# Joined score calls, earlier maxima and exponentials, and PSUM banks by expected end of reading, in a decoder's cross attention

## What is computed

```python
q = (queries @ wq_w + wq_b).reshape(B, S, H, DK)            # H = 16, DK = 64, S = 256
k_ext = concat([keys @ wk_w + wk_b, mk])                    # 256 + 128 = 384 keys
v_ext = concat([values @ wv_w + wv_b, mv])
scores = einsum('bhsd,bhtd->bhst', q, k) / sqrt(DK)
out = einsum('bhst,bhtd->bhsd', softmax(scores), v)
x = _layernorm(x + out @ wo_w + wo_b)
```

## Time and profile before

| | us |
|---|---|
| median of 3 runs | 1592.1 |
| lowest and highest run | 1581.37, 1595.23 |
| the profiled execution | 1586.94 |
| its span, first to last instruction | 1585.2 |

### The profile page before, as it was taken

One profiled execution on the slowest core, in us unless ns is written; L12 is line 12 of the kernel. 1 busy time (PEld: TensorE's weight loads), 2 busy tenths in 40 slices (PEclk: granted clock), 3 DMA queues, 4 the chain that ended last, 5 costly groups with the idle time before them and its releaser, 6 DMA issues.

```text
span 1585.2 us, 27670 instructions
## 1 busy us (share of the span) xinstructions
PE 1390.1 (88%) x9268; PEld 1122.7 (71%) x9268; DVE 1102.7 (70%) x2434; ACT 934.6 (59%) x2307; POOL 822.9 (52%) x862
## 2 busy tenths in 40 slices
PE   4778999999999999956999999689999979997891
PEld 3556777777777777654999999345555548997881
DVE  4677876666666666557788874688899963666635
ACT  4666565655655655542688861367778834466653
POOL 3664454444444444432688862287778750074640
PEclk9888999999999999956999999889999986998996
DMA  4100000000000000036556668634344402244574
GB/s 146 41 28 7 28 8 8 2 8 1 8 8 1 8 2 1 1 142 259 186 209 214 240 207 303 228 113 155 121 140 138 141 23 81 87 167 160 198 243 177
DMA packets 52942, 167.85 MB, mean 106 GB/s; under 512 B 13178, under 2 KB 22340, under 8 KB 44996
## 3 DMA queue, kind: packets, MB, share of 16 engines
q1 hardware_dynamic: 45316, 145.63, 26.1%
q0 software_dynamic: 7488, 20.46, 4.1%
HBM read 149.28 MB, written 16.78 MB: 105 GB/s over the span
## 4 chain that ended last, share of the span: by engine, by line
PE 34%; DVE 8%; issue 5%; ACT 5%; POOL 4%; DMA 2%; POOLq 0%; DVEq 0%; ACTq 0%; SPq 0%
PE m_ps L1713 10%; PE m_ps L1736 9%; POOL s_hc L2010 2%; DVE s_h L2345 2%; PE m_ps L1710 2%; PE s_yps L2410 2%; PE m_ps L1731 2%; ACT s_dps L2081 1%; PE m_ps L1693 1%; PE m_ps L1633 1%; DMA m_xrow<-table,m_row_from 1%; PE s_yps L2497 1%; PE m_ps L1643 1%; DVE tokens L1600 1%; PE m_ps L1661 1%
## 5 line engine op out<-in xcount | busy, mean ns | idle before, releaser
L306 POOL TENSOR_TENSOR a_pexp<-a_pexp,a_rsum 128x384 f32<-128x384 f32 (+1 forms) x320 | 246.0, 787 | 303.5 <-DVE a_rsum L523 303.5
L396 ACT ACTIVATE a_pexp<-a_ps,a_nmax 128x384 f32<-128x384 f32 (+1 forms) x320 | 180.8, 565 | 171.8 <-DVE a_nmax L519 171.3
L1713 PE MATMUL m_ps<-m_xT,m_w1s 128*128 128x256 f32 x1344 | 211.7, 296 | 18.0 <-issue 14.7
L1736 PE MATMUL m_ps<-m_w2s,m_hs 128*128 128x256 f32 x1344 | 203.4, 288 | 1.9 <-DVE m_hs L1532 1.9
L519 DVE TENSOR_REDUCE a_nmax<-a_ps 128x1 f32<-128x384 f32 (+1 forms) x320 | 153.8, 522 | 71.8 <-PE a_ps L620 70.7
L1713 PEld LDWEIGHTS m_ps<-m_xT,m_w1s 128*128 128x128 f32 x1344 | 186.4, 201 | 22.1 <-issue 17.3
L1736 PEld LDWEIGHTS m_ps<-m_w2s,m_hs 128*128 128x128 f32 x1344 | 181.5, 196 | 2.8 <-DVE m_hs L1532 1.7
L2010 POOL TENSOR_TENSOR s_hc<-s_h,s_bc_rows 128x1024 f32<-128x1024 f32 x64 | 150.9, 2361 | 61.0 <-DVE s_h L2345 59.0
L1096 POOL DMA_INDIRECT m_xrow<-table,m_row_from x78 | 81.5, 1044 | 142.0 <-DVE m_row_from L1431 107.0
L2345 DVE TENSOR_TENSOR_SCAN s_h<-s_dps,s_inp 128x512 f32<-128x512 f32 x128 | 148.7, 1203 | 0.0
L636 PE MATMUL a_ps<-a_ident,a_pexp 128*128 128x128 f32 x896 | 144.7, 274 | 3.4 <-ACT a_pT L255 3.0
(11 more groups left out here) (402 smaller groups left out, 3409.7 us busy)
## 6 DMA issues: line engine op xcount, KB each, us to landing
s_bc_rows<-s_bc_table SPq DMA_DIRECT2D x64, 512.0 KB, 3.7
arrived<-in_down SPq DMA_DIRECT2D x29, 1024.0 KB, 6.5
arrived<-in_up SPq DMA_DIRECT2D x23, 1024.0 KB
m_w<-in_up SPq DMA_DIRECT2D x24, 512.0 KB
m_w<-in_down SPq DMA_DIRECT2D x24, 512.0 KB
arrived<-results SPq DMA_DIRECT2D x3, 1024.0 KB, 8.4
m_fin<-results SPq DMA_DIRECT2D x4, 768.0 KB
tokens<-in_x SPq DMA_DIRECT2D x8, 256.0 KB, 6.8
```

Of the source, the lines that this page charges most:

```text
L306: nc.gpsimd.tensor_tensor(pexp[:, r, 0:n], pexp[:, r, 0:n], rsum[:, r:r + 1].to_broadcast([128, n]), ALU.mult).then_inc(normed, 1)
L396: nc.scalar.activation(pexp[:, r, 0:n], ps_s[score_bank(u)][:, 0:n], ACT.Exp, bias=nmax[:, r:r + 1], accum_out=sums[:, r:r + 1]).then_inc( ...
L1713: last = nc.tensor.matmul(ps_hid[ft % RING], w1s[wb][wp][:, k, of], xT[:, j % 2, xp, k, :], start=(k == 0 and wp == 0 and xp == 0), stop=( ...
L1736: last = nc.tensor.matmul(ps_y[j % 2][:, s, :], hs[hp][:, ft % RING, s * 128:(s + 1) * 128], w2s[wb][wp][:, ft, :], start=(ft == 0 and s = ...
```

## The change

1. In cross attention two score calls are joined: `scores(v)` and `scores(v + 2)` are both issued at the first step of a group, twelve matmuls in a row, and four banks (0 to 3) take them.
2. The maxima of the group's units 2 and 3 move from step 2 to step 1, and the exponentials of units 2 and 3 from steps 2 and 3 to steps 1 and 2.
3. T, pv and the jobs share banks 4 to 7 in cross attention. The planner gives out the bank whose reading it expects to end first, at 1.8 steps after a job's last part, 1.9 after a T and 2.3 after a pv. In self attention T has bank 4 and pv bank 3 (before 3 and 4).
4. q4, q5 and q6 move from steps 11, 16 and 17 to 6, 8 and 11, q7 from 18 to 17, x1T from 19 to 18.

```diff
-        ps = [ctx.enter_context(nc.psum_tensor(f"a_ps{n}", [128, 512], fp32)) for n in range(8)]
-        ps_s, PT_BANK, LAST_PT_BANK = ps[0:3], 3, 4
+        ps_all = ctx.enter_context(nc.psum_tensor("a_ps", [128, 8, 512], fp32))
+        ps = [ps_all[:, n, :] for n in range(8)]
+        SELF_PT_BANK, SELF_PV_BANK = 4, 3
...
-        score_bank = lambda u: u % 3
+        score_bank = lambda u: u % 3 if u < NS else u % 4
...
-        pt_bank = lambda n: ps[PT_BANK if n < NS // 2 else PT_BANK + n % 2]
...
+        def scores_at(v):
+
+            return (v,) if 0 <= v < NS and v % 2 == 0 else (v, v + 2) if NS <= v < UNITS and v % 4 == 0 else ()
+
+        def maxima_at(v):
+
+            if 0 <= v < NS:
+                return (v, v + 1) if v % 2 == 0 else ()
+            return {0: (v, v + 1), 1: (v + 1, v + 2)}.get(v % 4, ()) if NS <= v < UNITS else ()
+
+        def exponentials_at(v):
+
+            if 0 <= v < NS:
+                return (v,)
+            return {0: (v,), 1: (v, v + 1), 2: (v + 1,), 3: ()}[v % 4] if NS <= v < UNITS else ()
...
-            for at, kind, b in ((0, "k6", i), (1, "k7", i), (2, "q3", i), (11, "q4", i), (16, "q5", i), (16, "ctxT", i + 1), (17, "q6", i),
-                                (18, "q7", i), (19 if i >= 0 else 17, "x1T", i + 1), (19, "k0", i + 1), (20, "k1", i + 1), (21, "k2", i + 1), (22, "k3", i + 1),
+            for at, kind, b in ((0, "k6", i), (1, "k7", i), (2, "q3", i), (6, "q4", i), (8, "q5", i), (11, "q6", i), (16, "ctxT", i + 1),
+                                (17, "q7", i), (18 if i >= 0 else 17, "x1T", i + 1), (19, "k0", i + 1), (20, "k1", i + 1), (21, "k2", i + 1), (22, "k3", i + 1),
                                 (23, "k4", i + 1), (24, "q0", i + 1), (29, "q1", i + 1), (30, "k5", i + 1), (31, "q2", i + 1)):
...
-        FIXED = {"qk0": 6, "qkT0": 6, "qk1": 7, "qkT1": 7, "xnT": 5, "vs": 5, "oself": 5, "pv": LAST_PT_BANK}
+        FIXED = {"qk0": 6, "qkT0": 6, "qk1": 7, "qkT1": 7, "xnT": 5, "vs": 5, "oself": 5, "pv": SELF_PV_BANK}
...
-        last_in, order, busy_to = {}, {5: -3, 6: -2, 7: -1}, {}
+        last_in, order, read_by = {}, {4: -4, 5: -3, 6: -2, 7: -1}, {}
...
-            for kind, b, part, parts in JOBS_AT.get(v, []) + ([("pv", m, 0, 1)] if m is not None else []):
+            u = pt_at(v)
+            POOLED = (4, 5, 6, 7) if v >= NS + T_LAG else (5, 6, 7)
+            for kind, b, part, parts in JOBS_AT.get(v, []) + ([("pt", u, 0, 1)] if u is not None else []) + ([("pv", m, 0, 1)] if m is not None else []):
                 if part == 0:
-                    if kind in FIXED and v <= SHARED_TO:
+                    if kind == "pt" and u < NS:
+                        bank = SELF_PT_BANK
+                    elif kind in FIXED and v <= SHARED_TO:
                         bank = FIXED[kind]
                     elif v < HELD_TO:
                         bank = 5
                     else:
-                        bank = min((5, 6, 7), key=lambda n: (busy_to.get(n, FIRST) >= v, order[n]))
+                        bank = min(POOLED, key=lambda n: (read_by.get(n, FIRST), order[n]))
                     BANK[kind, b] = bank
                     BEFORE[kind, b] = last_in.get(bank)
                     last_in[bank] = (kind, b)
                     order[bank] = len(BANK)
-                    busy_to[bank] = v + parts - 1
+                    read_by[bank] = v + parts - 1 + {"pt": 1.9, "pv": 2.3}.get(kind, 1.8)
...
+            elif kind == "pt":
+                eng.wait_ge(pt_copied[pt_of(b) % 2], pt_of(b) // 2 + 1)
...
-                    if 0 <= v < UNITS:
-                        exponentials(v)
+                    for u in exponentials_at(v):
+                        exponentials(u)
...
-                    if u >= 2:
-                        pe.wait_ge(exped, u - 1)
+                    if u < NS:
+                        if u >= 2:
+                            pe.wait_ge(exped, u - 1)
+                    else:
+                        pe.wait_ge(exped, max(u - 2, NS))
+                        if u == NS + 2:
+                            pe.wait_ge(o_split, LAST_IN_SELF_PV_BANK + 1)
...
-                    if 1 <= n <= NS // 2:
-                        pe.wait_ge(pt_copied[(n - 1) % 2], (n - 1) // 2 + 1)
-                    elif n == NS // 2 + 1:
-                        pe.wait_ge(o_split, LAST_IN_PT_BANK + 1)
-                    elif n >= 2:
-                        pe.wait_ge(pt_copied[n % 2], n // 2)
+                    if BEFORE["pt", u] is not None:
+                        wait_drained(pe, BEFORE["pt", u])
...
-                    if v % 2 == 0 and 0 <= v < UNITS:
-                        scores(v)
+                    for u in scores_at(v):
+                        scores(u)
```

More of the change, by code:

```diff
@@ L111, in attention_layers @@
         by_nd = lambda a: a.rearrange("p (t d) -> p t d", t=ND)
-        score_bank = lambda u: u % 3
+        score_bank = lambda u: u % 3 if u < NS else u % 4
         pt_of = lambda u: u // 2 if u < NS else NS // 2 + u - NS
         pts_of_pair = lambda m: 2 * m + 2 if m < SELF_PAIRS else NS // 2 + 4 * m + 4 - NS
-        pt_bank = lambda n: ps[PT_BANK if n < NS // 2 else PT_BANK + n % 2]
         keys_of = lambda u: S if u < NS else KEYS
+        assert NS % 4 == 0
+        def scores_at(v):
[8 more added lines that the diff above has]
+            return {0: (v,), 1: (v, v + 1), 2: (v + 1,), 3: ()}[v % 4] if NS <= v < UNITS else ()
         def pt_at(v):
@@ L175, in attention_layers @@
                     order[bank] = len(BANK)
-                    busy_to[bank] = v + parts - 1
-                if part == parts - 1 and kind != "pv":
+                    read_by[bank] = v + parts - 1 + {"pt": 1.9, "pv": 2.3}.get(kind, 1.8)
+                if part == parts - 1 and kind not in ("pt", "pv"):
                     NUMBER[kind, b] = len(NUMBER)
@@ L181, in attention_layers @@
                         HIGH[kind, b] = len(HIGH)
-        LAST_IN_PT_BANK = max(b for kind, b in BANK if kind == "pv" and BANK[kind, b] == LAST_PT_BANK)
+        LAST_IN_SELF_PV_BANK = max(b for kind, b in BANK if kind == "pv" and BANK[kind, b] == SELF_PV_BANK)
         CHUNKS = [("wo0", 0, 2)] + [("wk", c, 5 + 3 * c) for c in range(4)] + [("mk", c, 16 + 2 * c) for c in range(2)] \
@@ L254, in copy_pt @@
             if u < NS:
-                copy(pT[:, m % 2, :, 0:ND, tok(s)], pt_bank(n)[:].rearrange("p (h k s) -> p h k s", h=2, k=ND)).then_inc(pt_copied[n % 2], 1)
+                copy(pT[:, m % 2, :, 0:ND, tok(s)], ps[BANK["pt", u]].rearrange("p (h k s) -> p h k s", h=2, k=ND)).then_inc(pt_copied[n % 2], 1)
             else:
-                copy(pT[:, m % 2, u % 2, :, tok(s)], pt_bank(n)[:, 0:KEYS].rearrange("p (k s) -> p k s", k=KX)).then_inc(pt_copied[n % 2], 1)
+                copy(pT[:, m % 2, u % 2, :, tok(s)], ps[BANK["pt", u]][:, 0:KEYS].rearrange("p (k s) -> p k s", k=KX)).then_inc(pt_copied[n % 2], 1)
         with nc.Block() as block:
@@ L395, in exponentials @@
                         act.wait_ge(pt_raw, pt_of(u - RING) + 1)
-                    nc.scalar.activation(pexp[:, r, 0:n], ps_s[score_bank(u)][:, 0:n], ACT.Exp, bias=nmax[:, r:r + 1],
+                    nc.scalar.activation(pexp[:, r, 0:n], ps[score_bank(u)][:, 0:n], ACT.Exp, bias=nmax[:, r:r + 1],
                                          accum_out=sums[:, r:r + 1]).then_inc(exped, 1)
@@ L515, in _ @@
                     t, r = v // U0, v % U0
-                    if v % 2 == 0 and 0 <= v < UNITS:
-                        for u in (v, v + 1):
-                            dve.wait_ge(scores_raw, u + 1)
-                            nc.vector.tensor_reduce(nmax[:, u % RING:u % RING + 1], ps_s[score_bank(u)][:, 0:keys_of(u)], AX.X, ALU.max, negate=True).then_inc(maxed, 1)
+                    for u in maxima_at(v):
+                        dve.wait_ge(scores_raw, u + 1)
+                        nc.vector.tensor_reduce(nmax[:, u % RING:u % RING + 1], ps[score_bank(u)][:, 0:keys_of(u)], AX.X, ALU.max, negate=True).then_inc(maxed, 1)
                     u = v - R_LAG
@@ L619, in scores @@
                             of = slice(64 * h, 64 * h + 64)
-                            last = nc.tensor.matmul(ps_s[score_bank(u + h)][:, 0:n], q[a][of, tok(s)], k[b][of, :], start=(a == 0 and b == 0), stop=(b == 1))
+                            last = nc.tensor.matmul(ps[score_bank(u + h)][:, 0:n], q[a][of, tok(s)], k[b][of, :], start=(a == 0 and b == 0), stop=(b == 1))
                             if b == 1:
@@ L635, in transpose_weights @@
                         for k in range(keys_of(u) // 128):
-                            last = nc.tensor.transpose(pt_bank(n)[:, at + k * 128:at + k * 128 + 128], pexp[:, g % RING, k * 128:k * 128 + 128], ident[:])
+                            last = nc.tensor.transpose(ps[BANK["pt", u]][:, at + k * 128:at + k * 128 + 128], pexp[:, g % RING, k * 128:k * 128 + 128], ident[:])
                     last.then_inc(pt_raw, 1)
```

## The result

| | before | after |
|---|---|---|
| median of the runs (11 each), us | 1591.72 | 1597.51 |
| the profiled execution, us | 1586.94 | 1594.79 |
| its span, us | 1585.2 | 1593.0 |

The changed kernel is slower by 0.5%: the ratio is 1.0051, with a 95% interval from 1.0032 to 1.0070. In the profiled executions the difference is 7.9 us.

The account below looks back on a forecast made before the run. TensorE issuing its list was taken as the bound (60.74 of 61.77 us busy). Gains 27.5 + 9.4 against losses of some 45 made +8.5 us: 1595.4 profiled, 1600.5 median; own range 1590 to 1611, overall 1572 to 1618.

Parts of the forecast that it names:

- saved per group (G3): Joined score call in each four-step group of cross attention: 0.43 us saved, over 64 groups -27.5 us.
- J1's low part: Low-part reading of the job in a group's second step: to start at 4.87 us, behind two maxima and a second exponential.
- J3: Job of a group's fourth step: takes the second step's job's bank, so starts at 5.41 us instead of 4.38.
- G0, G5, G7: First, sixth and eighth of a batch's eight four-step groups: waits for a low part of 1.03, 1.03 and 0.79 us.
- k0 starts, G4: Job k0 in a batch's fifth group: waits 2.12 us for q7's bank; that group loses 2.79 in all, lasting 9.1.
- light group: Three groups of the last batch, not bound by TensorE: 6.06 us for 5.20, +0.86 three times.
- The first rival: Job readings in cross attention end by 4.38 us, so all new waits go: 36.9 us gained, 1555 us; chance 0.20.
- The second: Second score call in the joined call fills anew: only 0.20 us saved per group, +14.7, 1615 us; chance 0.15.
- G4 of the last batch: Fifth group of the batch without next k and v: predicted to win 0.72 us.
- T3: Transpose of a group's fourth step: comes 1.16 us after the reciprocal behind two maxima; lateness costs a full batch 0.24.
- The two old waits: q4's wait at step 11 and the weighted values' at step 19: both go with the moved jobs, -1.34 us a batch.
- The other stages: Self part and mixture layers outside cross attention: not touched, so a gain or loss passes on whole.

Follow-up runs that it names:

- last experiment: Only the jobs moved, on the kernel before: ratio 0.9997; its reverse, only the jobs moved back, on the changed kernel: 1.0030 of the kernel before.

## Why the prediction was right

The predicted 1600.5 us stands against 1597.51, the predicted 0.5% against 0.5%. By its steps (us):

| step | predicted | measured |
|---|---|---|
| joined call to the next product | 1.23 | 1.27 |
| saved per group (G3) | 0.43 | 0.40 |
| J1's low part starts, G5 | 4.87 | 4.85 |
| J3 starts, G5 | 5.41 | 5.39 |
| G0, G5, G7 | 8.07, 8.07, 7.83 | 8.05, 8.08, 7.81 |
| k0 starts, G4 | 6.12 | 6.05 |
| G4 | 9.1 | 8.94 |
| full batch | 62.9 | 62.6 |
| light group | 6.06 | 6.08 |
| whole kernel, profiled | +8.5 | +7.9 |

Why it came so near: every link of the chain had a row, and the chain is in series, so there was nothing to guess but the order. The part that carried it was to follow the planner's choices to the bank that J3 gets, and to set real times against its steps. The planner counts in steps of equal length; after the join, the two steps from J1 to J3 last 2.08 us, and the two from J3 on nearly 5. The first rival (readings end in time) needed J1's low part at 4.4. It started at 4.85. The second (the call fills anew) needed 1.46 for the joined call.

The misses, all of them small:

- The saving per group. Pairs stand 0.18 apart as predicted, and I took 1.23 where the steps summed to 1.27. 64 groups make 1.9 us less gain.
- G4 of the last batch. Predicted 0.72 shorter than its 6.77 of before, it is 6.71. I had left out that the normalisation at step 16 also delays the maxima there, and with them the reciprocal and T3: 4.19 + 0.65 + 0.42 + 1.44 = 6.70. With the normalisation a step earlier (and the third maximum later) that group is 5.94.
- Batch 0 gained 1.2 us, not 0.3 (59.26 us for 60.44, from one G0 to the next).
- The links of the chain. The prediction says that both maxima stand ahead of J1's low part. Its times need only the first, and the trace shows only that one in the chain, with exponential 2 behind it.
- The two old waits. The prediction has both go by the move of the jobs. The one at step 19 did; the one at step 11 went by the planner's new rule and its pool (last experiment). The 1.34 us fit, but one of their two causes was wrong.
- The other stages. The start of cross attention is 1.7 us earlier (177.82 for 179.56), and what stands behind the start of its last weighted values is 1.8 longer. With the same self part, that start lies between 177.8 and 179.9 in the profiles of the experiments. The two cancel: cross attention alone is 7.7 us longer.
- Two groups lost 1.6 us to the clock (last section); without it cross attention would be 6.2 us longer, where +8.5 was predicted. So terms that were off by one to two us each cancelled in part. The form of the sum is shown by the groups; that the total agrees to 0.6 us is partly luck.

The light group shows the link from the maxima to T3 as the prediction had it, in the order of time of VectorE, GpSimd and TensorE:

```profile
660.60 0.15 DVE L545 RECIPROCAL a_rsum<-a_sums 128x2 f32<-128x2 f32 x1
...
660.83 3.18 POOL L329 TENSOR_TENSOR a_pexp<-a_pexp,a_rsum 128x384 f32<-128x384 f32 x4 [2.90 <-DVE a_rsum L545]
...
661.72 0.55 PE L659 MATMUL a_ps<-a_ident,a_pexp 128*128 128x128 f32 x3 [1.69 <-POOL a_pexp L329]
```

The reciprocal comes 3.04 us after the group's start (657.56), GpSimd 0.23 later, T3 at 4.16. There the earlier maxima hurt: TensorE had idle time in this group already before, so a later T3 makes the group longer at once.

The Trainium skill (TensorEngine Tiling (Array Packing), PSUM Bottleneck) says that tiling speeds up TensorE but not the evacuation of PSUM. Here banks did decide, not matmuls, but not because the readers were full: VectorE was busy 5.27 of 8.08 us in G5 and 6.35 of 8.94 in G4. What lacked was a bank while the chain of readers ran.

## What to carry to other kernels

A planner that gives out buffers by expected end of use should count in time, not in steps, as soon as a change makes the steps unequal (argued from the chain; no run tried such a planner): a join makes the steps behind it short, exactly where buffers come back. When a buffer is taken from a shared pool, walk the longest chain of readers (here maximum, exponential, high part, low part) from the engine that fills it, and see what the in-order engines hold ahead of it; moving instructions behind the reading, here a maximum and two exponentials whose results are needed later, was worth 3 us in 62, and the trace shows exponential 2 as the one that counted (it wasn't moved alone). And a product moved from one full step to another saved nothing, and in the changed kernel it took away what had filled a wait (0.5 us a batch).

## What the runs showed of the chip that I had not expected

In G4 of batch 2 of the changed kernel the wait for q7's low part is as long as in the other batches, but this time the granted clock fell behind it. The wait and the weighted values in TensorE's order of time, and the clock in the windows view:

```profile
336.36 0.39 PE L617 MATMUL a_ps<-a_cT_high,a_wk_high 128*128 128x256 f32 x1 [1.72 <-DVE a_qs_low L499]
...
337.80 2.83 PE L677 MATMUL a_ps<-a_pT,a_vx 128*64 128x256 f32 x12
```

```profile
330.31:336.36 6.05, 4.27 (x38) 3.54 (x36) 4.24 (x11) 4.08 (x13) 2.55 (x4) 1.00 0.15 43
...
337.80:340.56 2.76, 2.76 (x13) 1.38 (x13) 0.95 (x2) 0.05 (x1) 1.51 (x2) 0.50 0.00 0
```

The weighted values ran at 0.50 of the full clock, which is the 1.2 GHz level, and took 2.76 us to the next call for 1.45: a group of 10.25 us for 8.94. The group behind it lost another 0.24 (8.32 for 8.08, granted clock 0.96). Before the fall TensorE had been busy 4.27 of 6.05 us. So this wait, when the clock fell behind it, cost 1.6 us more. It happened once in the seven batches of this profile that have such a G4, each with 1.9 us idle but the first with 1.3. The joined kernel with the old readers (1.9 us idle in G4 or more) shows it in three batches, and the one with scores not joined and four shared banks (1.7 idle) in two, with groups of 10.12 and 10.05 us; their profiled times hold that loss. The kernel before and the other versions, with 1.5 us idle or less in G4, keep the full clock in every G4. What decides whether it falls was not tried.
